# Attention followed by a routed feed-forward block: rounded weights copied on chip, the hand-over between the two stages reordered, and result pieces loaded into another buffer

## The reference

```python
q, k, v = (einsum('bse,hed->bhsd', x, W) + b for W, b in ...)   # 16 heads of 64
attn = softmax(where(causal, q @ k.T / 8, -inf))
x = layernorm(x + concat_heads(attn @ v) @ Wo + bo)
res = x
xn = layernorm(x) * gamma + beta
w, idx = top_k(softmax(xn @ router_w.T / 1.5), 2)               # 8 experts, 2 per token
y = silu(xn @ W1[e]) @ W2[e]                                    # 128 -> 512 -> 128
x = layernorm(res + sum of the two gated y)
```

## Time and profile before

| what | value |
|---|---|
| time, median of 3 runs | 1269.91 us (1268.1 to 1270.12) |
| time of the profiled execution | 1270.98 us |
| its span in the trace | 1269.2 us |
| PE, busy share of the span | 98% |
| ACT, DVE, POOL, busy share | 88%, 83%, 59% |
| mean granted clock of PE | 0.998 of full speed |

### The profile page before, as it was taken

The page is one execution under the profiler, slowest core; times in us unless marked ns, Lnnn a source line. Parts: engine busy times, 40 slices in busy tenths (PEclk is TensorE's granted clock), DMA queues, the critical chain, the costliest instruction groups (busy, mean ns, idle before and its releaser), DMA issues.

```text
span 1269.2 us, 35973 instructions
## 1 busy us (share of the span) xinstructions
PE 1244.1 (98%) x11020; PEld 1112.8 (88%) x11020; DVE 1054.5 (83%) x5231; ACT 1117.4 (88%) x3470; POOL 753.3 (59%) x1325
## 2 busy tenths in 40 slices
PE   7999999999999999999999999999999899999997
PEld 6888888888888888888888888888888799999996
DVE  6888888888888888888888888888889786568885
ACT  7899999999999989999889999888888789999994
POOL 2246666666555555555555555555555777557776
PEclk9999999999999999999999999999999999999999
DMA  5000000000000000000000000000004223244553
GB/s 215 6 14 23 23 23 23 23 23 23 15 15 15 14 17 17 19 16 17 14 15 15 15 14 14 14 15 14 14 15 154 99 85 92 80 116 145 151 169 131
DMA packets 49212, 60.95 MB, mean 48 GB/s; under 512 B 8304, under 2 KB 35059, under 8 KB 48768
## 3 DMA queue, kind: packets, MB, share of 16 engines
q1 hardware_dynamic: 39376, 41.44, 10.5%
q0 software_dynamic: 8640, 17.13, 4.2%
q10 hardware_dynamic: 1008, 0.08, 0.1%
HBM read 30.72 MB, written 28.81 MB: 47 GB/s over the span
## 4 chain that ended last, share of the span: by engine, by line
PE 94%; ACT 2%; DVE 2%; issue 1%; DMA 0%; POOL 0%; SPq 0%; ACTq 0%; POOLq 0%; DVEq 0%
PE ps_a L1424 15%; PE ps_s L1467 13%; PE ps_s L1446 11%; PE ps_s L1424 8%; PE ps_f L1502 7%; PE ps_b L1459 7%; PE ps_f L1459 6%; PE ps_b L1718 5%; PE ps_a L1718 5%; PE ps_s L1449 4%; PE ps_b L1424 4%; PE ps_f L1424 3%; PE ps_a L1523 1%; PE ps_s L1477 1%; ACT f_y L777 1%
## 5 line engine op out<-in xcount | busy, mean ns | idle before, releaser
L777 ACT ACTIVATE f_y<-f_y,neg_max 128x256 f32<-128x256 f32 x512 | 256.4, 501 | 45.6 <-DVE neg_max L1074 45.5
L1074 DVE CUSTOM_DVE_ANT_0 f_y<-ps_s,mask 128x256 f32<-128x256 f32 x512 | 214.5, 419 | 63.5 <-PE ps_s L1449 63.2
L1424 PE MATMUL ps_a<-xt_hi,weights 128*128 128x256 f32 x1024 | 242.8, 300 | 0.0
L667 POOL TENSOR_TENSOR ot_lo<-f_y,ot_hi 128x512 fp32r<-128x512 f32 x128 | 164.8, 1287 | 116.3 <-PE ps_s L1449 111.0
L1090 DVE TENSOR_SCALAR f_y<-f_y,inv_sums 128x256 f32<-128x256 f32 x512 | 194.7, 380 | 6.9
L780 ACT ACTIVATE f_y<-f_y,neg_max 128x128 f32<-128x128 f32 x512 | 199.6, 390 | 0.0
L1467 PE MATMUL ps_s<-ident,f_y 128*128 128x128 f32 x1536 | 195.3, 274 | 0.0
L1424 PEld LDWEIGHTS ps_a<-xt_hi,weights 128*128 128x128 f32 x1024 | 175.7, 189 | 16.0 <-issue 10.8
L742 POOL DMA_INDIRECT y_tok<-f_y,m_dest x142 | 146.3, 1031 | 67.5 <-DVE m_dest L1277 38.1
L1446 PE MATMUL ps_s<-qk 64*128 64x256 f32 x1024 | 176.5, 421 | 5.6 <-ACT pt L825 2.5
L1467 PEld LDWEIGHTS ps_s<-ident,f_y 128*128 128x128 f32 x1536 | 172.2, 141 | 4.9 <-issue 0.5
(11 more groups left out here) (254 smaller groups left out, 3338.8 us busy)
## 6 DMA issues: line engine op xcount, KB each, us to landing
m_x<-queue SPq DMA_DIRECT2D x71, 133.0 KB, 2.3
f_y<-y_tok SPq DMA_DIRECT2D x32, 256.0 KB, 3.3
queue<-empty SPq DMA_DIRECT2D x8, 532.0 KB
x_raw<-in_x SPq DMA_DIRECT2D x32, 128.0 KB
out_x<-f_y SPq DMA_DIRECT2D x16, 256.0 KB, 3.3
y_tok<-f_y,m_dest POOLq DMA_INDIRECT x142
f_y<-in_w SPq DMA_DIRECT2D x1, 2048.0 KB, 11.3
m_w<-in_w SPq DMA_DIRECT2D x1, 2048.0 KB, 15.2
```

What stands on the lines that cost most here:

```text
L667: pool.tensor_tensor(ot_lo[:, first:first + 2, :], ot[:, s % 2], ot_hi[:, first:first + 2, :].bitcast(F32), ALU.subtract).then_inc(ot_lo_d ...
L777: act.activation(row[:, 0:2 * P], row[:, 0:2 * P], ACT.Exp, scale=-1.0, bias=neg_max[:, pair, h, 0:1], accum_out=sums[:, d % 2, pair, h, 0:1])
L1074: dve.tensor_tensor_reduce(out=row[:, 0:2 * P], in0=ps_s[:, pair, h, 0:2 * P], in1=mask[:].rearrange("p a b -> p (a b)"), scale=-1.0, scal ...
L1424: ins = pe.matmul(dst, lhs, rhs, start=(i == 0), stop=(i == len(terms) - 1))
```

## The change

The rounded weights no longer go to DRAM: SP copies `w1_part` on chip to `w1_hi`, the place of the raw `W1`, once POOL has made the rest, and the four loads go. At the end of attention POOL does `slots` and `send_tokens` of sequence 31 before it splits groups 124 and 125, and waits for all probabilities ahead of the first split. PE transposes the first expert rows before the last `z`, does `hidden(0)` whole ahead of `outputs(LAST - 1)`, and takes six pairs' projection in step 0 and two in step 1 (four and four before). ACT's `copy_outputs(LAST - 1)`, `expert_weights(1)` and `router_exponentials(SEQS)` stand inside step 0. Pieces are loaded into four buffers `f_raw` in the place of attention's weights and summed into six buffers `f_norm`.

```diff
+        f_norm = early_use[:, 0:FBUFS * FIN * D].rearrange("p (f d) -> p f d", f=FBUFS)
+        w1_hi = early_use[:, 9 * HD:9 * HD + E * HID]
+        f_raw = weights[:, 2 * HD:6 * HD].bitcast(F32).rearrange("p (f k d) -> p f k d", f=FRAW, k=TOP)
...
-                    sp.wait_ge(w1_hi_done, e + 1)
-                    sp.dma_start(w1_rounded[:, e * HID:(e + 1) * HID], w1_part[:, e % 2]).then_inc(w1_stored[e % 2], 16)
+                    sp.wait_ge(w1_lo_done, e + 1)
+                    sp.dma_start(w1_hi[:, e * HID:(e + 1) * HID], w1_part[:, e % 2]).then_inc(w1_stored[e % 2], 16)
...
-            for par in range(2):
-                sp.wait_ge(w1_stored[par], E // 2 * 16)
-            sp.wait_ge(v_ready, SEQS * 4)
-            for part in range(4):
-                cols = slice(part * E * HID // 4, (part + 1) * E * HID // 4)
-                sp.dma_start(weights[:, W1_HI:W1_LO].bitcast(F32)[:, cols], w1_rounded[:, cols]).then_inc(w1_hi_loaded, 16)
...
-                if f >= FBUFS:
-                    sp.wait_ge(f_out_stored[f % FBUFS], f // FBUFS * 16)
+                if f >= FRAW:
+                    if f - FRAW < EARLY:
+                        sp.wait_ge(g_sum_done, f - FRAW + 1)
+                    else:
+                        sp.wait_ge(f_sum_ready, f - FRAW - EARLY + 1)
...
-            for s in range(LAST - 4, LAST - 2):
-                round_outputs(s)
-                rest_of_outputs(s)
             slots(SEQS - 1)
             send_tokens(SEQS - 1, 0)
-            for s in range(LAST - 2, LAST):
+            pool.wait_ge(probs_done, LAST * 2)
+            for s in range(LAST - 4, LAST):
                 round_outputs(s)
                 rest_of_outputs(s)
...
             expert_weights(0)
-            copy_outputs(LAST - 1)
-            expert_weights(1)
-            router_exponentials(SEQS)
...
                 if j == 0:
+                    copy_outputs(LAST - 1)
                     affine(1)
+                    expert_weights(1)
+                    router_exponentials(SEQS)
...
+                act.wait_ge(f_out_stored[(f + EARLY) % FBUFS], (f + EARLY) // FBUFS * 16)
...
                 dve.wait_ge(f_y_loaded[f], TOP * 16)
+                if f >= FBUFS:
+                    dve.wait_ge(f_out_stored[f % FBUFS], f // FBUFS * 16)
...
+                        transpose_x(0)
                         pe.wait_ge(z_done, n)
                         pe.wait_ge(ot_done, LAST - 2)
...
-                        transpose_x(0)
...
-            hidden(0, range(0, 2))
+            hidden(0)
             pe.wait_ge(ot_done, LAST - 1)
             outputs(LAST - 1)
-            hidden(0, range(2, CH))
...
-                    output_projection(SEQS, range(0, 4))
+                    output_projection(SEQS, range(0, 6))
                 if j == 1:
-                    output_projection(SEQS, range(4, PAIRS))
+                    output_projection(SEQS, range(6, PAIRS))
```

More of the change, by code:

```diff
@@ L27 @@
 FBUFS = 6
+FRAW = 4
 EARLY = 11
@@ L224, in postln_block @@
         m_xlo = sb("m_xlo", [P, 2, ROWS], F32R)
-        m_tanh = [early_use[:, at * HD:at * HD + CH * ROWS].rearrange("p (c t) -> p c t", c=CH) for at in (9, 15)]
-        m_h = early_use[:, 10 * HD:10 * HD + 2 * CH * ROWS].rearrange("p (a c t) -> p a c t", a=2, c=CH)
-        m_xf = early_use[:, 12 * HD:12 * HD + 2 * ROWS].rearrange("p (a t) -> p a t", a=2)
+        m_tanh = [early_use[:, at * HD:at * HD + CH * ROWS].rearrange("p (c t) -> p c t", c=CH) for at in (3, 15)]
+        m_h = early_use[:, 4 * HD:4 * HD + 2 * CH * ROWS].rearrange("p (a c t) -> p a c t", a=2, c=CH)
+        m_xf = sb("m_xf", [P, 2, ROWS])
         m_y = early_use[:, 14 * HD:14 * HD + YBUFS * ROWS].rearrange("p (a b d) -> p a b d", a=YBUFS, b=BLOCKS)
@@ L492, in load_outputs @@
                     sp.wait_ge(m_y_sent[buf], ((steps_until(f) - 1 - buf) // YBUFS + 1) * BLOCKS * 16)
[L493 to L494 removed]
+                if f >= FRAW:
[3 more added lines that the diff above has]
+                        sp.wait_ge(f_sum_ready, f - FRAW - EARLY + 1)
                 for k in range(TOP):
[L496 removed]
+                    sp.dma_start(f_raw[:, f % FRAW, k, :], y_parts[k, f]).then_inc(f_y_loaded[f], 16)
             def store_outputs(f):
@@ L502, in store_outputs @@
                     sp.wait_ge(f_out_done, f + 1 - EARLY)
-                sp.dma_start(out_parts[f], f_buf[:, f % FBUFS, 0, :]).then_inc(f_out_stored[f % FBUFS], 16)
+                sp.dma_start(out_parts[f], f_norm[:, f % FBUFS, :]).then_inc(f_out_stored[f % FBUFS], 16)
             for j in range(NJ):
@@ L895, in expert_weights @@
                 if j == 0:
-                    act.wait_ge(w1_hi_loaded, 4 * 16)
+                    for par in range(2):
+                        act.wait_ge(w1_stored[par], E // 2 * 16)
                     act.wait_ge(w1_lo_done, E)
@@ L900, in expert_weights @@
                 col = act.value_load(tab_w[0:1, j:j + 1], min_val=0, max_val=(E - 1) * HID)
-                ins = act.activation(m_w1[:, j % 2, 0], weights[:, bass.ds(col + W1_HI, HID)].bitcast(F32), ACT.Copy)
+                ins = act.activation(m_w1[:, j % 2, 0], w1_hi[:, bass.ds(col, HID)], ACT.Copy)
                 if j < LATER:
@@ L938, in _ @@
                 act.wait_ge(f_shift_done, f + 1)
+                act.wait_ge(f_out_stored[(f + EARLY) % FBUFS], (f + EARLY) // FBUFS * 16)
                 for i in range(FIN):
                     cols = slice(i * D, (i + 1) * D)
-                    ins = act.activation(f_buf[:, (f + EARLY) % FBUFS, 0, cols], f_sum(f)[:, cols], ACT.Identity,
+                    ins = act.activation(f_norm[:, (f + EARLY) % FBUFS, cols], f_sum(f)[:, cols], ACT.Identity,
                                          scale=f_r[:, f % 2, i:i + 1], bias=f_shift[:, f % 2, i:i + 1])
@@ L1317, in piece_sum @@
             def piece_sum(f):
-                both = f_buf[:, f % FBUFS]
                 dve.wait_ge(f_y_loaded[f], TOP * 16)
-                dve.tensor_tensor(both[:, 0, :], both[:, 0, :], both[:, 1, :], ALU.add).then_inc(g_sum_done, 1)
+                if f >= FBUFS:
+                    dve.wait_ge(f_out_stored[f % FBUFS], f // FBUFS * 16)
+                dve.tensor_tensor(f_norm[:, f % FBUFS, :], f_raw[:, f % FRAW, 0, :], f_raw[:, f % FRAW, 1, :], ALU.add
+                                  ).then_inc(g_sum_done, 1)
             def piece_statistics(f):
@@ L1324, in piece_statistics @@
                 for i in range(FIN):
-                    ins = dve.bn_stats(g_stats[:, i, :], f_buf[:, f % FBUFS, 0, i * D:(i + 1) * D])
+                    ins = dve.bn_stats(g_stats[:, i, :], f_norm[:, f % FBUFS, i * D:(i + 1) * D])
                 ins.then_inc(g_stats_done, 1)
@@ L1340, in piece_scale @@
                 for i in range(half * FIN // 2, (half + 1) * FIN // 2):
-                    cols = f_buf[:, f % FBUFS, 0, i * D:(i + 1) * D]
+                    cols = f_norm[:, f % FBUFS, i * D:(i + 1) * D]
                     ins = dve.tensor_scalar(cols, cols, g_mv[:, par, i, 0:1], g_r[:, par, i:i + 1],
@@ L1787, in _ @@
                 for k in range(TOP):
-                    ins = pe.matmul(f_sum(f), ident[:], f_buf[:, (f + EARLY) % FBUFS, k, :], start=(k == 0),
+                    ins = pe.matmul(f_sum(f), ident[:], f_raw[:, (f + EARLY) % FRAW, k, :], start=(k == 0),
                                     stop=(k == TOP - 1))
```

4 lines of the change are left out of this document (removed).

## The result

| | median, lowest to highest, runs |
|---|---|
| before | 1269.88 us, 1267.52 to 1272.49, 16 |
| changed | 1272.40 us, 1270.59 to 1273.15, 16 |
| ratio | 1.0020, 95% interval 1.0014 to 1.0027 |

The profiled execution of the changed kernel took 1272.06 us (before: 1270.98), with a span of 1270.2 (1269.2). The forecast for the median was 1270.7. Measured, the changed kernel's median lies 2.5 us above before's instead of 0.8; the interval of the ratio lies wholly above 1.

What follows compares the result with a forecast made beforehand. It took PE as the bound, with 94% of the chain, so only its waits could move: hand-over +0.8 us, tail nothing, profiled execution 1271.8, less the 1.07 offset a median of 1270.7 us. Range 1266.3 to 1273.6.

Steps and rivals of the forecast that it cites:

- likeliest case: Whole kernel: POOL's split delays ACT's copy and the clock falls, median 1270.7 us, reaching from 1268.9 to 1272.3; chance 0.55.
- hand-over: From attention to experts, about 984 to 1009 us: 0.7 to 0.85 us later, taken as +0.8.
- the sum: Profiled execution of 1270.98 us plus 0.8 makes 1271.8 us.
- the tail: End of the kernel, pieces 13 and 15: nothing gained, with a slack of 0.6 us.
- The loads: First expert rows land by 986.2, so PE's 2.26 us idle time and the low clock behind it go.
- POOL's new order: Slots and sends, 4.6 us, precede the split of group 124; ACT copies group 126 at 994.1, `hidden(0)` starts 0.5 later.
- The clock: Behind PE's 5.6 us idle time before `hidden(0)`, the granted clock falls to 0.50: loss 1.5 us, upper end 2.6.
- To `hidden(1)`: From `hidden(0)` through ACT's copy, `affine(1)` and weights, with 0.3 for DVE: `hidden(1)` at 1004.5, 1.15 us later.
- rule on two-port modes: DVE in two-port modes and GpSimd exclude each other; sends would begin at 989.9, the sum staying at +0.8 us.
- To step 2: PE's transposes of the projection wait for ACT's `out_t` to 1008.9; they began just before 1008.2 in the kernel before.
- The sends: Rival: POOL's sends stall beside DVE, 1.6 us each, giving 1272.3 or 1273.9; slower chance 0.17 together with clock and tail.
- From the profile to the median: Profiled execution lies 1.07 us above the median of 1269.91, so 1271.8 becomes a median of 1270.7 us.

Runs made afterwards that it cites:

- e3: Changed kernel with before's order on POOL, ACT and PE, leaving only on-chip copies, missing loads and new buffers: 1268.51 us against before's 1270.56, ratio 0.9984.
- e1: Changed kernel with POOL's old order, groups 124 and 125 split ahead of slots and sends, no added wait: 1266.11 us against before's 1270.56, ratio 0.9964.
- e2: Kernel before with POOL's new order and nothing else of the change: 1271.67 us against before's 1270.56, ratio 1.0011.
- e5: Kernel before with nine filler calls on PE ahead of the transposes of the first expert rows: 1269.33 us against before's 1270.38, ratio 0.9991.
- e9: Kernel before, unchanged, profiled again: 1270.42 us. Its theory: low clock in only part of the executions, those without it below 1269.5 us.
- e6: Changed kernel with POOL splitting groups 124, 125 and 126 before slots and sends, no added wait: 1266.24 us against before's 1270.38, ratio 0.9970.
- e7: Changed kernel with POOL splitting all four groups 124 to 127 before slots and sends: 1266.85 us against before's 1270.38, ratio 0.9973.
- e12: Changed kernel with POOL splitting only group 124 before slots and sends, no added wait: 1266.42 us against before's 1269.69, ratio 0.9974.
- e4: Changed kernel with 20 filler calls on PE behind the last transposes of probabilities: 1270.58 us against before's 1270.56, ratio 1.0002.

## Why the prediction was right or wrong

Its likeliest case came true, with its sign and its chain. The size was 0.8 and is 2.5 in the medians, where about half of it is explained, and 1.15 in the trace's hand-over. The median, 1272.40, lies just above 1272.3, to which the likeliest case was said to reach, and inside the range. For the profiled execution the sum gave 1271.8 and 1272.06 was measured; that this is so near is in part luck, as attention ended 0.37 later than in before's profile and the tail gave 0.35 back, and neither was in the sum.

- **The loads.** Right: `m_x` landed before PE came, `outputs(126)` took 1.5, and its whole gain went into PE's next wait. e3 shows that it was worth 2.0 us by itself, less than the end of the idle time and clock loss it removes, as a later wait pays the clock again.
- **POOL's new order.** Right, shown by e1 and e2. ACT's copy came 7.16 behind the end of attention, forecast 994.1 - 987.49 = 6.6: the slot rows and the two sends took 4.94 together, not 4.6, and the split 1.96. `hidden(0)` made it up: forecast 9.5, measured 9.59. PE's idle time was forecast at 5.6 and is 5.53.
- **The clock.** Right in kind, mis-sized: "I take 1.5, nearest to the one stretch that is seen". The loss is 1.7 to 1.9. The low stretch began within the idle time and was 6.8 us long where before's was 3.4, so 3.6 us of it were left when PE had work again. The term was sized from a row in which the low stretch began about when the work did.
- **To `hidden(1)`.** Forecast 17.0 behind the end of attention, measured 17.44: 0.3 more in the low stretch and 0.1 behind it, where I had allowed DVE's rest of x 0.3 of delay. It took

```profile
1003.77 1.39 DVE L1299 TENSOR_TENSOR m_xlo<-m_xf,m_xhi 128x256 fp32r<-128x256 f32 x1 [2.07 <-ACT m_xhi L885]
```

  in the changed kernel, beside POOL's split of group 127, and 0.43 at 989.68, where POOL had only small slot rows. The Trainium skill, SBUF — State Buffer, section "Who interferes with whom", says that a DVE instruction with two inputs in SBUF contends with a GpSimd instruction that reads SBUF; this is such a pair, and the trace agrees. Its rule on two-port modes, which the prediction drew on, agrees as well: with POOL's splits moved away the last two narrow scalings took 0.29 and 0.27 us, in place of 1.29. That the scaling runs in such a mode, no trace shows.
- **To step 2.** ACT's `out_t` did come last, at 1009.07 + 0.39. `hidden(2)` starts 1.52 later than before's 1008.41; 0.37 of that was there when attention ended. The hand-over costs 1.15, forecast 0.8: most of the difference is the clock's. Over both profiles of the changed kernel and all four of before it is 1.21.
- **The sends** did not stall (0.30 between them), and **the tail** gave nothing up to the end of the engines' work, as forecast; the 0.35 behind the last store was not forecast.
- **From the profile to the median.** The step that missed most: "It lies 1.07 above the median of 1269.91, so for the median I forecast 1270.7". I took the offset of before's one profiled execution to hold for the changed kernel. But it is the chance of one execution: before's runs spread over 5 us and more. The changed kernel's profiled executions (1272.06, 1271.78) lie 0.3 and 1.0 below its medians, before's four (1270.98, 1270.42, 1271.39, 1270.22) lie on average 0.2 to 1.1 above the five medians measured of it. The mean of two less the mean of four is 1.17. In the spans it is 1.07: the hand-over's 1.21, 0.37 more between `hidden(2)` and the fillers, 0.36 less in the tail and 0.16 less before the end of attention. The medians differ by 2.5 and 2.35.

So half of the loss is shown and half is not: no kept trace has the other 1.3 us. Six single executions can't rule it out either. The runs' standard deviations are 0.7 us for the changed kernel and 1.1 to 1.9 for before, by which 1.17 is uncertain by 0.7 to 1.1 us (one standard error, an estimate).

Every timed run has its mean granted clock on record, and that speaks against the guess that the changed kernel loses more clock in runs without a trace. Its 27 runs show 0.995 to 0.997, on average 0.9958, as its two profiles do (0.995 and 0.996). Before's 74 runs show 0.9972 on average, its profiles 0.997 and 0.998. But before's spread does go with the clock:

| before, on the chip of e1: mean granted clock | runs | mean time |
|---|---|---|
| 0.999 | 9 | 1269.1 us |
| 0.997 and 0.998 | 19 | 1270.4 us |
| 0.992 to 0.996 | 7 | 1273.9 us |

In before's profile 3.4 us of low clock at the hand-over and 2.4 at the end make 0.998; 0.999 has room for 3.8 us at most. So by estimate the low stretch at the hand-over is missing in the runs at 0.999, which are 12 of the 74. They are 1.3 us faster than those at 0.997 and 0.998 on this chip and 0.7 on that of e5, of the order of its price. That gives the theory of e9 a small part back, and e5's narrow spread fits it, but 12 runs of 74 don't move the median by 1.3 us. The landing of the scatter near 1026 (0.9 us between its two lengths) is another part that varies. Where the other half of the loss lies stays open.

The versions e1, e6, e7 and e12 beat both kernels, by 0.26% to 0.36% of before's time; they can't be told from one another. The cheapest mend is e1's: leave POOL's two splits where they were.

## What to carry to other kernels

Moving work ahead on an in-order engine is priced by who waits for what it overtakes: here 4.6 us of sends overtook a split of 1.9 that freed a buffer, and cost 6 to 7 us because the waiter had just become able to use it. A gain and a loss at one place are not added but hidden in each other, so test the parts of such a change apart: together they made 0.2% slower, apart 0.16% faster and 0.1% slower (this one not clear of noise), and all but one of the parts 0.36% faster. Don't carry one profiled execution's offset to the median over to another kernel; take more than one profile, and look for waits over the whole span, not only around the change.

## What the runs showed that I had not expected

- The granted clock falls during an idle time and stays low well after it: it fell at about 994.3, with PE idle since 991.9, and was back only at about 1001.1, with PE busy since 997.45. In e3 it fell behind two waits of 0.98 and 1.40 with little work between them, and in e12 behind one of 1.85 near 1024; behind waits of 1.80 to 2.05 at the same place it stayed at 1.00 in four other profiles.
- Attention, in which only the copies of the rounded weights differ, ended at 987.21 to 988.59 in the profiles. In the first profile of the changed kernel the granted clock was 0.90 from 10 to 20 us and 0.93 from 20 to 30; in its second 1.00, and attention ended 0.59 sooner. Such a low stretch of 3.4 us from about 18 us on is in four of the fourteen profiles (also e2, e4 and e12).
- Filler matmuls in a 2.26 us wait of the kernel before cost nothing and gave 0.09% (interval 0 to 0.18%).
